# Attention stage: nine slots per pair, token chunks transposed over thirteen steps, and the loop over pairs written out

## The reference

```python
h = _L0_tok_ref(...)                       # (16, 128, 1024)
h = jnp.concatenate([h, txt], axis=1)      # (16, 205, 1024)
h = h + attn(_layernorm(h), Wqkv, Wo)      # 32 heads of 32, one shared k and v
h = h + ffn(_layernorm(h), ...)            # base matmul + routed low-rank experts

def attn(x):                               # ALiBi and a causal mask
    qkv = x @ Wqkv                         # 1024 -> 1024 (q) + 32 (k) + 32 (v)
    scores = q k^T * 32**-0.5 + slopes * (pos_k - pos_q), masked
    return (softmax(scores) @ v) @ Wo
```

## Time and profile before

| | before |
|---|---|
| median of 3 runs | 1719.29 us (1718.76 to 1721.86) |
| the profiled execution | 1722.0 us, its span 1720.2 us |
| PE busy | 1502.7 us (87%) |
| PEld busy | 1334.9 us (78%) |
| DVE busy | 1136.6 us (66%) |
| ACT busy | 739.5 us (43%) |
| POOL busy | 514.4 us (30%) |
| mean granted TensorE clock | 0.941 |

### The profile page before, as it was taken

How to read it: one execution, slowest core, us unless ns; L and a number is a source line. 1 busy time by engine, 2 the same in 40 slices (tenths; PEclk the granted TensorE clock), 3 DMA queues, 4 the chain that set the end, 5 groups by cost and what they waited for, 6 DMA issues and landing times. The chain is left out here.

```text
span 1720.2 us, 31628 instructions
## 1 busy us (share of the span) xinstructions
PE 1502.7 (87%) x9700; PEld 1334.9 (78%) x9700; DVE 1136.6 (66%) x4142; ACT 739.5 (43%) x2624; POOL 514.4 (30%) x314
## 2 busy tenths in 40 slices
PE   0254389999999999999999868999999999999999
PEld 0254388787878878887888747999899899998997
DVE  7999277978788787978787856444444454444443
ACT  3355247776777776776787731010111111101100
POOL 1787314354434344444444411001011010010110
PEclk9887689999999999999999669999999999999999
DMA  6134445445454444445464541121121211211211
GB/s 202 37 87 96 104 94 83 98 81 100 74 104 74 109 74 80 98 79 99 79 128 75 123 150 59 54 74 49 61 73 37 73 63 47 73 49 61 74 33 40
DMA packets 110527, 139.63 MB, mean 81 GB/s; under 512 B 13156, under 2 KB 96484, under 8 KB 110040
## 3 DMA queue, kind: packets, MB, share of 16 engines
q1 hardware_dynamic: 110408, 138.41, 35.1%
HBM read 62.82 MB, written 40.30 MB: 60 GB/s over the span
## 5 line engine op out<-in xcount | busy, mean ns | idle before, releaser
L700 ACT ACTIVATE P<-P,nmax 128x128 f32<-128x128 f32 (+1 forms) x1024 | 434.3, 426 | 92.5 <-DVE nmax L790 86.2
L764 POOL TENSOR_TENSOR P<-P,rden 128x512 f32<-128x512 f32 (+1 forms) x256 | 329.2, 1308 | 452.8 <-DVE rden L796 452.6
L790 DVE CUSTOM_DVE_ANT_0 P<-sc,mask 128x128 f32<-128x128 f32 (+1 forms) x1024 | 292.3, 323 | 98.7 <-PE sc L612 92.5
L1129 POOL TENSOR_TENSOR h<-h,base_b 128x1024 f32<-128x1024 f32 (+1 forms) x26 | 62.9, 2418 | 639.2 <-DVE xn L1156 639.2
L802 DVE COPY PTR<-pt 128x282 f32<-128x282 f32 x512 | 222.5, 435 | 35.2 <-PE pt L622 21.3
L642 PE MATMUL pr<-xT_hi,wq_hi 128*128 128x410 f32 x576 | 242.3, 421 | 0.0
L1040 PE MATMUL b<-w_hi,x2T_hi 128*128 128x390 f32 (+3 forms) x624 | 214.7, 344 | 1.0 <-DVE x2T_lo L1166 1.0
L1040 PE MATMUL b<-w_lo,x2T_hi 128*128 128x390 f32 (+3 forms) x624 | 212.9, 341 | 0.0
L1040 PE MATMUL b<-w_hi,x2T_lo 128*128 128x390 f32 (+3 forms) x624 | 212.5, 341 | 0.0
L642 PE MATMUL pr<-xT_lo,wq_hi 128*128 128x410 f32 x576 | 203.4, 353 | 0.0
L642 PE MATMUL pr<-xT_hi,wq_lo 128*128 128x410 f32 x576 | 202.4, 351 | 0.0
(11 more groups left out here) (174 smaller groups left out, 3064.5 us busy)
## 6 DMA issues: line engine op xcount, KB each, us to landing
Qs<-q_hi SPq DMA_DIRECT2D x128, 205.0 KB, 4.7
Qs<-q_lo SPq DMA_DIRECT2D x64, 205.0 KB, 5.5
att_dram<-att SPq DMA_DIRECT2D x64, 205.0 KB, 2.3
at<-att_dram SPq DMA_DIRECT2D x25, 512.0 KB, 4.7
h<-h_dram SPq DMA_DIRECT2D x25, 512.0 KB, 3.3
out<-h SPq DMA_DIRECT2D x25, 512.0 KB, 2.6
h_dram<-Y SPq DMA_DIRECT2D x64, 128.0 KB, 3.1
ht<-h_dram SPq DMA_DIRECT2D x16, 512.0 KB, 5.9
```

The lines of the kernel that those rows point to most:

```text
L700: last = nc.scalar.activation(P[rows, j % 2, i, cols], P[rows, j % 2, i, cols], ACT.Exp, scale=-1.0, bias=nmax[at], accum_out=den[at])
L764: lastp = nc.gpsimd.tensor_tensor(w, w, r, ALU.mult)
L790: lastv = v.tensor_tensor_reduce(P[0:n, j % 2, i, cols], sc[i % 2][0:n, cols], mask[0:n, m], 1.0, 3.0e38, ALU.add, ALU.min, nmax[0:n, j % ...
L1129: nc.gpsimd.tensor_tensor(h2[0:n, par, :], h2[0:n, par, :], base_b[0:n, :], ALU.add).then_inc(biased, 1)
```

## The change

There are three parts.

**Nine slots.** The LN slot is gone. The slots hold q0, q1, q2, kv, q3, ..., q7, and scores lie in slots 5 to 8 and in slots 0 to 3 of the next pair (9 to 12). Slot 4 alone has no scores.

**LN transposes spread out.** A group is now one chunk of 128 features for all four tiles (four transposes, 410 columns). The chunks of the *next* pair follow the main work at steps 0, 1, 3, 4, 6 of slot 8 and steps 0, 2, 4 of slot 0: thirteen steps. ScalarE copies a chunk one step later and VectorE two steps later, ahead of that step's scores. The chunks use banks 0, 1, 0 and then bank 1 five times; the products alternate between banks 0 and 1, and q7 and the transposed v have bank 2. Pair 0's eight chunks come ahead of all slots, over three banks. Each kind of use has semaphores of its own. VectorE's statistics start at step 14 and the scaling at step 38.

**No loop.** All eight pairs are written out on every engine; waits on counts in registers become waits on constants.

```diff
-SLOTS = 10
+SLOTS = 9
-    MAIN = ["ln", ("q", 0), ("q", 1), "kv", ("q", 2), ("q", 3), ("q", 4), ("q", 5), ("q", 6), ("q", 7)]
+    MAIN = [("q", 0), ("q", 1), ("q", 2), "kv", ("q", 3), ("q", 4), ("q", 5), ("q", 6), ("q", 7)]
+    MAIN_BANK = [0, 1, 0, 1, 0, 1, 0, 1, 2]
+    VT_BANK = 2
+    LN_SLOT = SLOTS - 1
+    LN_AT, LN_BANK, FIRST_BANK = [0, 1, 3, 4, 6, 8, 10, 12], [0, 1, 0, 1, 1, 1, 1, 1], [i % BANKS for i in range(KC)]
+    def ln_chunk(slot, i, after):
+        at = (slot - LN_SLOT) % SLOTS * GH + i - after
+        return LN_AT.index(at) if at in LN_AT else None
-    SCORE_SLOT = [5, 6, 7, 8, 9, 11, 12, 13]
+    SCORE_SLOT = [5, 6, 7, 8, 9, 10, 11, 12]
...
     def visit(body):
-        def run(eng):
-            body(0, True, False)
-            with eng.Fori(1, PAIRS - 1) as p:
-                body(p, False, False)
-            body(PAIRS - 1, False, True)
+        def run():
+            for p in range(PAIRS):
+                body(p, p == 0, p == PAIRS - 1)
             body(PAIRS, False, None)
...
+            def turn_ln(p, i):
+                banks = banks_of(p)
+                if i == 0:
+                    pe.wait_ge(xn_ready, 4 * p + 4)
+                if banks[i] in banks[:i]:
+                    pe.wait_ge(ln_read, KC * p + max(k for k in range(i) if banks[k] == banks[i]) + 1)
+                else:
+                    wait_count(pe, main_read, SLOTS * p - 2 + banks[i])
+                for s, (c, t0, n) in enumerate(TILES):
+                    at = c * S + t0
+                    last = nc.tensor.transpose(pr[banks[i]][:, at:at + n], ht[0:n, s, i * 128:(i + 1) * 128], ident[0:n, 0:n])
+                last.then_inc(ln_turned, 1)
...
                         if main is not None:
                             main_step(p, slot, main, i)
+                        chunk, pair = ln_chunk(slot, i, 0), ln_pair(p, slot, first, last)
+                        if chunk is not None and pair is not None:
+                            turn_ln(pair, chunk)
                         if i == 6 and aj is not None:
                             values(*aj)
...
-        STATS_AT, RSTD_RATE = 12, 1
-        APPLY_AT, APPLY_EVERY = 36, 1
+        STATS_AT, RSTD_RATE = 14, 1
+        APPLY_AT, APPLY_EVERY = 38, 1
...
+            def lo_ln(p, i):
+                dve.wait_ge(ln_hi, KC * p + i + 1)
+                v.tensor_tensor(xT[1][:, i, :], pr[banks_of(p)[i]][:, 0:PT], xT[0][:, i, :].bitcast(F32), ALU.subtract).then_inc(ln_read, 1)
```

More of the change, by code:

```diff
@@ L559, in body @@
                 for slot, main, sj, tj, aj in slots(p, first, last):
+                    if slot == 1 and last is False:
+                        sp.wait_ge(ln_turned, KC * p + KC)
+                        for s in range(4):
+                            load_h(p + 1, s)
+                    if slot == 1 and last is True:
+                        sp.wait_ge(ln_turned, KC * p + KC)
+                        for k in range(4):
+                            load_wo(k)
                     if last is None and slot == 1:
@@ L580, in body @@
                         stack_q(p - 1, 7)
[L581 to L584, removed]
                     if aj is not None:
@@ L667, in main_step @@
[L667 to L671, removed]
+                        turn_v(p)
+                    if slot == 0:
+                        pe.wait_ge(ln_read, KC * p + last_in(banks_of(p), 0) + 1)
+                    elif slot == 1:
+                        pe.wait_ge(ln_read, KC * p + KC)
+                    elif slot == SLOTS - 1:
+                        pe.wait_ge(vt_read, p + 1)
+                    else:
+                        pe.wait_ge(main_read, SLOTS * p + slot - 1)
@@ L672, in main_step @@
+                if slot == 0 and i > last_in(banks_of(p), 0):
+                    pe.wait_ge(ln_read, KC * p + i + 1)
+                out = pr[MAIN_BANK[slot]][:, 0:PT]
                 if what == "kv":
-                    last = three(pr[use % BANKS][:, 0:PT], wkv, slice(0, 128), i)
+                    last = three(out, wkv, slice(0, 128), i)
                 else:
-                    last = three(pr[use % BANKS][:, 0:PT], wq, slice(128 * what[1], 128 * what[1] + 128), i)
+                    last = three(out, wq, slice(128 * what[1], 128 * what[1] + 128), i)
@@ L691, in _ @@
             pe.wait_ge(const_ready, 1)
-            visit(body)(pe)
+            for i in range(KC):
+                turn_ln(0, i)
+            visit(body)()
         @block.scalar
@@ L731, in body @@
                         if i == 0 and slot == 0 and not first:
[L732 to L737, removed]
+                            hi_part(p - 1, SLOTS - 1)
+                        if i == 0 and slot >= 1 and main is not None:
+                            hi_part(p, slot - 1)
+                        chunk, pair = ln_chunk(slot, i, 1), ln_pair(p, slot, first, last)
+                        if chunk is not None and pair is not None:
+                            hi_ln(pair, chunk)
                         if sj is not None:
@@ L749, in _ @@
             act.wait_ge(const_ready, 1)
-            visit(body)(act)
+            for i in range(KC):
+                hi_ln(0, i)
+            visit(body)()
         @block.gpsimd
@@ L862, in body @@
                     for i in range(GH):
+                        chunk, pair = ln_chunk(slot, i, 2), ln_pair(p, slot, first, last)
+                        if chunk is not None and pair is not None:
+                            lo_ln(pair, chunk)
                         if sj is not None:
@@ L909, in _ @@
                 ln_apply(0, s, link)
-            visit(body)(dve)
+            for i in range(KC):
+                lo_ln(0, i)
+            visit(body)()
 def mlp_block(nc, ctx, io, W):
```

123 lines of the change are left out of this document (50 added, 73 removed).

## The result

| | before | after |
|---|---|---|
| median of the runs | 1719.03 us | 1674.83 us (1673.85 to 1676.83) |
| the profiled execution | 1722.0 us, span 1720.2 | 1673.85 us, span 1672.1 |
| PE busy | 1502.7 us | 1471.7 us (88%) |
| DVE busy | 1136.6 us | 1137.9 us (68%) |
| mean granted TensorE clock | 0.941 | 0.96 |

The change is faster: the ratio is 0.9741 (95% interval 0.9724 to 0.9758), 44 us by the medians and 48 us between the two profiled executions. The forecast was 1670, in a range of 1654 to 1698.

A forecast was written before the change was run, and what follows sets the result against it. TensorE sets the pace in pairs 1 to 6, VectorE 13% behind. Pairs 1 to 6 -46, pair 7 -6, pair 0 -5, tail +8: -49 us from 1722.0, 1670 us by the median; range 1654 to 1698.

The forecast's parts named there:

- The jumps: Loop of pairs 1 to 6: five jumps back cost 4.4 us each in stall and slower clock; straight code saves 22 us.
- The transfer: Slot 7: unit 2's scores stop waiting for q3's last transfer, 2.2 us a pair, plus 1 to 1.5 for the clock.
- Rival 4: Slot 8: q6's copy waits for q4's transfers out of `q_hi`; 2 to 3 us a pair return, 1690 us; chance 0.09.
- The slots: Pairs 1 to 6: slots priced by like content sum to 88.3 us a pair against 96.0, a gain of 46 us.
- The chunk of 0.5 us: Slots 8 and 0: each of eight transpose chunks costs TensorE 0.5 us, 4.0 us a pair.
- The waits of the chunks: Second chunk waits for q6's low part and bank 1 chunks for each other: 0.5 us a pair added.
- VectorE's work in slots 3 to 5: Slot 3 takes 9.8 us with the root; slots 4 and 5 keep their content, at 7.8 and 9.3 us.
- small waits in the LN slot: Pairs 1 to 6: some 6 us of the 46 us gain comes from these waits going.
- Rival 1: Only stalls go; VectorE idles through values in slots 8 and 0 to 3, 4 us more a pair: 1694 us; chance 0.14.
- The tail: One more unit there: +4 us in slot 0, +1.5 and +2.5 in slots 1 and 2, +8 us in all.
- Pair 0: -5 us in all, including +1.5 because the first chunk needs all four tiles normed.
- The third rival: Clock falls to half in the thirteen steps with chunks, +93 us, about 1763 us; chance 0.06 together with another rival.

The follow-up runs named there:

- unrolled kernel: The kernel before with its ten slots, only the loop over pairs written out on every engine: 1696.59 us, ratio 0.9861.
- spread statistics: The changed kernel with the next pair's statistics, root and scaling spread over later steps (14 to 61): 1670.80 us.
- two tiles on GpSimd: The changed kernel with statistics thinned out, two of four tiles scaled by GpSimd and two by VectorE at steps 44 and 46: 1658.09 us.
- serial chunks: The changed kernel with the eight chunks at steps 0 to 7 of slot 8, all but the first in bank 1: 1714.02 us.
- dense chunks: The changed kernel with the eight chunks at steps 0 to 7 of slot 8, in banks 0 and 1 by turns: 1673.11 us.
- loop of nine slots: The changed kernel with its nine slots and spread chunks, but pairs 1 to 6 in a loop again: 1705.73 us.
- q3 late: The changed kernel with q3's three transfers held back until four heads of unit 1 are scored: 1706.61 us.

## Why the prediction was right

**The jumps: right.** Forecast 22 us, measured 24 by the unrolled kernel. The price of 4.4 us a jump, read from the same slot in the loop and in straight code, was 4.5 net. In the straight code neither VectorE's copies nor ScalarE's wait without a releaser, as pairs 0 and 7 had shown.

**The transfer: right.** No scores wait for it any more; slot 7 went from 12.6 us on the mean of pairs 1 to 6 (13.2 in the unrolled kernel) to 9.5, so 3.2 or 3.7 a pair where I had 3.2 to 3.7. Rival 4, a copy held up by the transfers in `q_hi`, appears once, in pair 0, and costs nothing.

**The slots: right in slots 0, 1, 6, 7 and 8 within 0.1 us, too high in slot 2 and too low in three others.** Taking a slot's time from a slot with the same content held. The chunk of 0.5 us held too: 2.5 us for the five in slot 8, as pair 7 without them shows. The waits of the chunks came as forecast, 0.5 us a pair, but they lie within the 23.1 us of slots 8 and 0; the sum had them twice.

**The term that was mis-sized is VectorE's work in slots 3 to 5.** I took these slots from slots 3 to 5 before, plus nothing for what moved into them. Measured are +0.8 (slot 3, forecast 9.8), +0.5 (slot 4) and +0.9 (slot 5), against -0.5 in slot 2: two steps of statistics now stand in slot 3 with the first six of the root, and two scalings, at steps 40 and 41, stand with scores and turns in slot 5, where all four stood in slot 4 before. The prediction counted statistics in slot 2 alone and said that slots 4 to 6 keep their content; both are wrong by its own start steps of 14 and 38. Six pairs of 1.2 us are the 7 us that pairs 1 to 6 fell short (-38.9, not -46). Put the other way: the prediction had some 6 us of the gain from small waits in the LN slot, and no such gain is left beside jump and transfer, since VectorE's work for the next pair costs 4.5 us a pair here and 3.3 in the unrolled kernel (its pairs 1 to 6 less its pair 7, slots 0 to 4). The experiments show the cause for slots 2, 3 and 5: with the scalings gone from slot 5 it takes 9.3 us, and with the statistics thinned slots 2 and 3 take 9.8 and 9.8 to 10.0. For slot 4 they don't: it takes 8.3 us also with no scaling in it, and 8.4 with the statistics moved; what holds it there stays open.

**Rival 1 fell in its mechanism.** It said that VectorE can't make up for the time in which it waits for TensorE's values. In a full slot without work for the next pair it does stand idle for 1.4 us there. But slot 2 of pair 4 (574.17 to 585.16) has VectorE busy for 10.83 of 10.99 us, slot 1 takes two steps of statistics at no cost (9.45 us, as in pair 7), and in the kernel with spread statistics slot 7 takes two scalings for 0.1 us. So a full slot has about 1.5 us of room, and VectorE sets slot 2's length by the sum of its work. In slots 4 and 5 it is busy for only 6.6 of 8.3 and 8.3 of 10.2 us and still costs time: there it matters in which step the work stands: two scalings at steps 40 and 41 cost slot 5 0.9 us, and two at steps 44 and 46 (two tiles on GpSimd) leave slots 5 and 6 at 16.7 us together, against 16.6 in pair 7. Of the 12.5 us of work for the next pair (75 us of instructions in pairs 1 to 6), 4.5 show.

**The tail: mis-sized, +2.6 for +8.** By the values' starts, from the last ones of pair 7 on, slot 1 and slots 2 and 3 together cost +1.7 and +2.3, near the forecast for slots 1 and 2 (+1.5, +2.5), but slot 0 only +0.9 in place of +4, and slots 4 and 5 gave back 1.7. That is +3.3 in all, 0.7 of it ahead of the table's boundary. To ScalarE's last copy the tail is 54.5 us, not near 60. Windows of before, slots 0 and 4, and then the same two of after:

```profile
954.60:965.00 10.40, 5.81 (x50) 4.09 (x49) 8.45 (x16) 6.45 (x14) 5.09 (x4) 0.81 0.54 87
987.90:1000.30 12.40, 7.68 (x43) 5.10 (x42) 9.97 (x21) 7.04 (x19) 6.04 (x4) 0.50 0.06 18
```
```profile
901.70:913.00 11.30, 8.06 (x64) 5.87 (x67) 9.86 (x40) 10.44 (x34) 5.06 (x4) 0.86 0.84 126
940.00:951.20 11.20, 5.08 (x43) 3.47 (x42) 10.14 (x22) 6.91 (x19) 6.18 (x5) 0.83 0.06 19
```

In slot 0 VectorE had been idle for 2 of 10.4 us, which the new maskings filled in part, and its first two Wo pieces took 1.97 and 2.21 us before and 1.47 and 1.72 after. Slot 4 now runs at a clock of 0.83 where it had 0.50. Why either is so was not tried. That the two errors have opposite signs is luck, and it made the sum look better than its terms: 7 us too much gain in the pairs, 5 us too much loss in the tail.

**Pair 0.** -6.6 for -5. Its first chunk does wait for all four tiles: from the start of the scaling to q0's first matmul it is 9.3 us, against 7.2 before (+2.1, forecast +1.5). Both begin at 219.2 only because the stage ahead ended 2.2 us earlier in this execution. Counted from the scaling, pair 0 moved by -4.4, not -6.6, and 2.2 of the 48.1 us between the two profiled executions are not the change's; the medians have 44 against a forecast of 49.

**The third rival fell.** The granted clock is 1.00 over all of pairs 1 to 6, chunks included. The Trainium skill's sentence that transposes don't engage the full clock (TensorE: Matmul & The Clock Gate, Part 4: PE-mode transpose) doesn't hold here. In the other kernels the clock fell mostly where TensorE had stood idle for 1.8 us or more just before. The serial chunks are the exception: with waits of 0.7 us, one a step, it fell to 0.50 in slot 8 of two pairs of seven. That is the third rival's outcome, at waits that the change doesn't have. Pair 0 tests the sentence harder. In the changed kernel TensorE had been idle for 31.6 us and then ran nothing but its 32 transposes, from 219.17 to 224.8 us; the clock was 0.50 at first and 1.00 before they ended (the first product starts at 225.39):

```profile
219.20:222.20 3.00, 3.00 (x17) 2.77 (x18) 1.34 (x3) 1.54 (x3) 0.00 (x0) 0.50 0.00 0
223.70:225.20 1.50, 1.04 (x8) 0.64 (x8) 1.40 (x3) 1.35 (x3) 0.00 (x0) 1.00 0.00 0
```

The same happened with dense chunks and with spread statistics. In the kernel before, and when the changed kernel ran again, the clock stayed at 0.50 until after the first products.

## What to carry to other kernels

Read what a stretch will cost from a stretch of the same trace that has the same content, per slot and not per stage; it was good to 0.1 us where nothing else moved. Then list for each slot, step by step, what the second-busiest engine does in it, and follow every piece of work that a new start step moves: the same two scalings cost 0.1 us in one slot and 1.8 in another. And when a change has several parts, split its gain by an experiment for each: here the loop and one late transfer gave all of it, and the new arrangement of the slots none.

## What the runs showed of the hardware

- A jump back stalls VectorE for up to 2.7 us and ScalarE for up to 2.4 in the kernel before, and for up to 4.1 and 2.8 us in the loop of nine slots.
- Behind each of the five idle gaps of 3.9 us on TensorE (the jumps of the nine-slot loop) the granted clock fell to 0.50. Behind shorter gaps it fell sometimes: in four of eight of 2.2 to 2.8 us (q3 late), and in six of eight of 1.8 to 2.2 us (the unrolled kernel, whose slot 7 takes 11.6 to 14.8 us).
- It also fell to 0.50 with no single wait longer than 0.8 us, behind three to five waits of about 0.7 us, one a step (serial chunks, slot 8 of pairs 6 and 2; in the same slot of pairs 1, 3, 4 and 5, which has the same waits, it stayed at 1.00).
- The clock rose from 0.50 to 1.00 while TensorE ran nothing but transposes (pair 0 of the changed kernel, 219.2 to 225.2 us).
- GpSimd takes 3.8 to 3.9 us for a subtract and multiply of 128 x 1024 numbers by two values per partition; VectorE takes 0.8. A sum of that size takes GpSimd 2.4 us.
- The same scaling took VectorE 0.75 us in one slot and up to 1.30 in another (statistics spread).
